# A mixture-of-experts kernel: routed rows staged one tile ahead, copied by VectorE, with their row numbers copied by GpSimd

## What is computed

```
logits = x @ gate_w.T ; probs = softmax(logits)
topk_w, topk_i = top_k(probs, 2) ; topk_w = topk_w / sum(topk_w)
combine = sum(one_hot(topk_i, 8) * topk_w)
g = x @ w_gate[e] ; u = x @ w_up[e]           # 1024 -> 1408, for each expert e
eo = (silu(g) * u) @ w_down[e]                # 1408 -> 1024
out = sum over e of combine[:, e] * eo
out = out + sigmoid(x @ shared_gate) * shared_expert(x)
```

## Time and profile before

| | |
|---|---|
| three timed runs | 2174.4, 2179.98, 2189.42 us; median 2179.98 |
| the profiled execution | 2164.92 us, its slowest core's span 2163.4 us |
| spans of the eight cores | 2120.9 to 2163.4 us |
| TensorE matmuls busy | 2027.5 us, 94% of the span |
| VectorE, ScalarE, GpSimd busy | 789.7, 559.6 and 223.6 us |
| DMA | 258.35 MB, mean 119 GB/s |
| routed stage on core 7 | 1106.4 us to the end, 38 tiles |

### The profile page before, as it was taken

How to read it: one execution, slowest core, us unless ns; L and a number is a source line. 1 busy time by engine, 2 the same in 40 slices (tenths; PEclk the granted TensorE clock), 3 DMA queues, 4 the chain that set the end, 5 groups by cost and what they waited for, 6 DMA issues and landing times. The chain is left out here.

```text
span 2163.4 us, 37870 instructions; the slowest of 8 cores (2120.9 to 2163.4 us)
## 1 busy us (share of the span) xinstructions
PE 2027.5 (94%) x14227; PEld 1242.7 (57%) x14227; DVE 789.7 (37%) x1945; ACT 559.6 (26%) x967; POOL 223.6 (10%) x197
## 2 busy tenths in 40 slices
PE   6999999966979999999969999999999999999997
PEld 3444444432434444444437777777777767767775
DVE  5677777675325544555311111111111111111111
ACT  1333333321212112211202222223223232222222
POOL 1000000000210111011101111111111111111101
PEclk9999999977989999999989999999999999999999
DMA  9733334465773224322497868778677877777533
GB/s 200 135 99 97 98 98 98 117 131 121 132 200 117 89 109 157 117 89 109 124 182 115 132 105 131 118 115 134 114 128 120 134 112 127 131 111 129 94 54 50
DMA packets 260389, 258.35 MB, mean 119 GB/s; under 512 B 194201, under 2 KB 200604, under 8 KB 258082
## 3 DMA queue, kind: packets, MB, share of 16 engines
q0 software_dynamic: 55440, 140.28, 38.2%
q1 hardware_dynamic: 204818, 116.36, 21.8%
HBM read 219.65 MB, written 83.49 MB: 140 GB/s over the span
## 5 line engine op out<-in xcount | busy, mean ns | idle before, releaser
L1364 PE MATMUL ffn_ps<-r_xT,w 128*128 128x256 bf16 (+1 forms) x6688 | 687.3, 265 | 31.4 <-PEq L1198 31.4
L1364 PEld LDWEIGHTS ffn_ps<-r_xT,w 128*128 128x128 bf16 x6688 | 613.1, 98 | 109.8 <-issue 36.4
L1294 DVE TENSOR_TENSOR r_h<-r_si,ffn_ps 128x256 bf16<-128x256 bf16 (+1 forms) x418 | 165.9, 400 | 875.8 <-DVEq L1198 874.1
L1073 PE MATMUL ffn_ps<-xln2T,w 128*128 128x512 bf16 x1408 | 307.0, 380 | 2.5 <-DVE sh_h L1086 2.5
L1274 ACT ACTIVATE r_si<-ffn_ps 128x256 bf16<-128x256 f32 (+1 forms) x418 | 151.8, 367 | 425.5 <-ACTq L1198 422.7
L394 PE MATMUL att_ps<-xlnT,w 128*128 128x512 bf16 x1024 | 237.8, 382 | 1.2 <-DVE xlnT L348 1.1
L1073 PEld LDWEIGHTS ffn_ps<-xln2T,w 128*128 128x128 bf16 x1408 | 136.8, 98 | 166.0 <-issue 4.6
L1322 POOL DMA_INDIRECT out<-r_y,r_meta x70 | 111.0, 1586 | 695.0 <-POOLq L1198 657.9
L1374 PE MATMUL ffn_ps<-w,r_h 128*128 128x512 bf16 x770 | 169.3, 379 | 0.0
L1374 PE MATMUL ffn_ps<-xca,r_h 128*128 128x512 bf16 x770 | 169.3, 379 | 0.0
L394 PEld LDWEIGHTS att_ps<-xlnT,w 128*128 128x128 bf16 x1024 | 96.0, 98 | 116.0 <-issue 4.6
(11 more groups left out here) (152 smaller groups left out, 1121.1 us busy)
## 6 DMA issues: line engine op xcount, KB each, us to landing
xca<-x SPq DMA_DIRECT2D x48, 512.0 KB, 5.7
w<-wu POOLq DMA_DIRECT2D x16, 1408.0 KB, 13.3
w<-wg POOLq DMA_DIRECT2D x8, 2112.0 KB, 15.2
combT_d<-cb SPq DMA_DIRECT2D x8, 1024.0 KB, 4.9
x1b<-x SPq DMA_DIRECT2D x16, 512.0 KB, 5.2
out<-xca SPq DMA_DIRECT2D x16, 512.0 KB, 3.4
out<-x1b SPq DMA_DIRECT2D x16, 512.0 KB, 3.7
xca<-wd POOLq DMA_DIRECT2D x4, 2048.0 KB, 14.4
```

The costliest lines, as they stand in the source:

```text
L1073: i = q.matmul(b_, wslot[w][:, dt * IFF + it * C:dt * IFF + (it + 1) * C], xT2[t % 2][:, dt, :], start=(dt == 0), stop=(dt == 7))
L1294: v.tensor_mul(h[:, it, 0:rt], rsi[:, it % 4, 0:rt], bank(2 + it % 4)[:, RT:RT + rt]).then_inc(r_h, 1)
L1364: i = q.matmul(bank(2 + it % 4)[:, c0:c0 + rt], w_[:, dt * IFF + it * C:dt * IFF + (it + 1) * C], xT[:, dt, 0:rt], start=(dt == 0), stop=( ...
```

## The change

The rows are loaded into a new buffer `r_xTn`. VectorE copies it to `r_xT` at the start of each of its tiles, frees the new buffer (xfree) and tells TensorE with a new semaphore (xr). TensorE waits for xr and no longer frees anything. GpSimd copies the 128 row numbers of a half into a small buffer `r_ids` before each indirect DMA, which reads its numbers there; so meta is freed as soon as both DMAs are issued, ahead of the waits for their landing. In SBUF `r_xTn` takes the place that `r_xT` had, a buffer `r_skip` that nothing uses keeps `r_y` clear of `x1b`, and ScalarE's wait for the stores is gone. The tile sizes are as before.

```diff
@@ -1182,16 +1182,19 @@
         dn_done = (v_dn.h, v_dn.n)
         wout_done = wpe
 
-    xT = sb2("r_xT", [C, 8, RT], BF16)
+    xTn = sb2("r_xTn", [C, 8, RT], BF16)
     h = sb2("r_h", [C, NIT, RT], BF16)
     rsi = sb2("r_si", [C, 4, RT], BF16)
     meta_f = sb2("r_meta", [C, 2, (ROW - D) // 2], F32)
+    r_skip = sb2("r_skip", [C, 5 * D + 256], F32)
     ysb = sb2("r_y", [C, 2, D], F32)
+    xT = sb2("r_xT", [C, 8, RT], BF16)
     meta_i = meta_f[:, :, :].bitcast(I32)
-
-    r_xfull, r_xfree, r_gu, r_si, r_h, r_y, r_yfull, r_yfree, r_mfull, r_mfree, r_expert = (
+    ids = sb2("r_ids", [C, 2], I32)
+
+    r_xfull, r_xfree, r_xr, r_gu, r_si, r_h, r_y, r_yfull, r_yfree, r_mfull, r_mfree, r_expert = (
         es.enter_context(nc.semaphore("r_" + k)) for k in
-        ("xfull", "xfree", "gu", "si", "h", "y", "yfull", "yfree", "mfull", "mfree", "expert"))
+        ("xfull", "xfree", "xr", "gu", "si", "h", "y", "yfull", "yfree", "mfull", "mfree", "expert"))
     acc = [[sem("r_acc%d_%d" % (hf, e)) for e in range(8)] for hf in range(2)]
 
 
@@ -1215,7 +1218,7 @@
 
 
     def first_rows(s):
-        s.dma_start_transpose(out=xT[:, :, :], in_=dr["xs"].bitcast(BF16)[0:RT, 0:D]
+        s.dma_start_transpose(out=xTn[:, :, :], in_=dr["xs"].bitcast(BF16)[0:RT, 0:D]
                               ).then_inc(r_xfull, 16)
         s.dma_start(out=meta_f[:, :, :], in_=dr["xs"][0:RT, D // 2:ROW // 2].rearrange(
             "(b p) c -> p b c", p=C)).then_inc(r_mfull, 16)
@@ -1255,7 +1258,7 @@
         with s.Fori(1, total, 1):
             r = s.snap(row, min_val=0, max_val=8 * REG - RT)
             take(s, r_xfree)
-            s.dma_start_transpose(out=xT[:, :, :], in_=dr["xs"].bitcast(BF16)[bass.ds(r, RT), 0:D]
+            s.dma_start_transpose(out=xTn[:, :, :], in_=dr["xs"].bitcast(BF16)[bass.ds(r, RT), 0:D]
                                   ).then_inc(r_xfull, 16)
             take(s, r_mfree)
             s.dma_start(out=meta_f[:, :, :], in_=dr["xs"][bass.ds(r, RT), D // 2:ROW // 2].rearrange(
@@ -1265,7 +1268,6 @@
 
     def act_routed(a):
         wait(a, cnt_tok)
-        wait(a, out_stored[1])
         a.sem_inc(r_yfree, 1)
         for e, n, full in expert_tiles(a):
             def tile(rt):
@@ -1289,6 +1291,9 @@
         wait(v, cnt_tok)
         for e, n, full in expert_tiles(v):
             def tile(rt):
+                take(v, r_xfull, 16)
+                v.tensor_copy(xT[:, :, :], xTn[:, :, :]).then_inc(r_xfree, 1)
+                v.drain().then_inc(r_xr, 1)
                 for it in range(NIT):
                     take(v, r_si)
                     v.tensor_mul(h[:, it, 0:rt], rsi[:, it % 4, 0:rt],
@@ -1319,9 +1324,11 @@
 
             def add_rows(hf, i):
                 take(g, r_yfull)
+                g.tensor_copy(ids[:, hf:hf + 1], meta_i[:, hf, 0:1])
+                g.drain()
                 g.indirect_dma_start(
                     out=dr["out"],
-                    out_offset=bass.IndirectOffsetOnAxis(ap=meta_i[:, hf, 0:1], axis=0),
+                    out_offset=bass.IndirectOffsetOnAxis(ap=ids[:, hf:hf + 1], axis=0),
                     in_=ysb[:, hf, :], in_offset=None, compute_op=ALU.add
                 ).then_inc(acc[hf][e].h, 16)
 
@@ -1332,9 +1339,10 @@
                     add_rows(0, i)
                     with g.If_ne(half, i):
                         add_rows(1, i)
+                    g.sem_inc(r_mfree, 1)
+                    with g.If_ne(half, i):
                         g.wait_ge(acc[1][e].h, 16 * (i + 1))
                     g.wait_ge(acc[0][e].h, 16 * (i + 1)).then_inc(r_yfree, 1)
-                    g.sem_inc(r_mfree, 1)
                     g.reg_sub(left, left, 1)
                     next_part(e, i + 1)
             for i in range(2, 4):
@@ -1355,7 +1363,7 @@
             wg, wu, wd = wslot[sl], wslot[sl + 1], wslot[sl + 2]
 
             def tile(rt):
-                take(q, r_xfull, 16)
+                take(q, r_xr)
                 for it in range(NIT):
                     if it >= 4:
                         take(q, r_h)
@@ -1375,8 +1383,6 @@
                                          h[:, it, hf * C:(hf + 1) * C],
                                          wd[:, it * D + dc * 512:it * D + (dc + 1) * 512],
                                          start=(it == 0), stop=(it == NIT - 1))
-                            if hf == 0 and dc == 0 and it == 0:
-                                i.then_inc(r_xfree, 1)
                         i.then_inc(r_y, 1)
             tile_loop(q, n, full, tile)
     em("tensor", pe_routed)
```

## The result

| | before | changed |
|---|---|---|
| median of the timed runs | 2183.18 us (4 runs) | 2238.28 us (4 runs) |
| ratio, paired on one chip | | 1.0187, 95% interval 1.0124 to 1.0249 |
| the profiled execution | 2164.92 us | 2232.96 us |
| again on a second chip (`e2_again`) | | 2232.68 us, ratio 1.0238 (1.0179 to 1.0296) |

What follows compares the result with a forecast made beforehand. TensorE was taken as the bound, its idle time in the routed stage as winnable. -17.2 - 16.5 + 0.5 + 1.7 + 0.5 = -31.0 us takes the median 2179.98 to 2149 us, range 2135 to 2168.

Steps and rivals of the forecast that it cites:

- what is added: Costs of the change: VectorE's copy +0.5 us, clock behind the first gap +1.7, GpSimd's copy and drain +0.5.
- H+3.7: H is a half tile's start; GpSimd was to release meta (mfree) about 3.7 us after it.
- Rival 3: GpSimd's copy and drain dear, c us per copy, delaying meta and row loads: 2196 us at c = 7; chance 0.03.
- The first wait: TensorE's 15.45 us wait in the first routed tile goes, with 1.72 us of clock: -17.2 us.
- what is late next: With the first wait gone, the second tile's rows, issued about 1123, arrive by the need at about 1134.
- The small waits: TensorE's waits behind full and half tiles (4.7 and 8.3 us) and 5.0 of clock go, 1.5 stay: -16.5 us.
- VectorE's copy: Copying r_xTn to r_xT takes 1.26 us, hidden in 37 tiles, exposed in the first: +0.5 us, 0 to 1.
- Clock behind the first gap: After the 3.2 us gap before the first routed tile, core 7 may pay a lower clock: +1.7 us, 0 to 1.7.
- The sum: All terms on core 7: -31.0 us, from the median 2179.98 to 2149 us.
- Rivals 1, 2 and 4: After half tiles waits stay (2158 to 2167, 0.15); stage start transfer-bound (2154 to 2160, 0.11); ScalarE's wait merely replaced (2166, 0.04).

Runs made afterwards that it cites:

- e9_wait: The changed kernel with a semaphore in place of GpSimd's drain, and ScalarE's wait for the last stores put back: 2164.68 us, ratio 0.9948.
- e1_sem: The changed kernel, with a semaphore after GpSimd's copy of the row numbers in place of the drain: 2149.21 us, ratio 0.9899.
- e4_store: The kernel before, with only the results' staging moved and ScalarE's wait for the stores taken out: 2178.33 us, ratio 1.0012.
- e5_noids: The changed kernel without the row numbers' copy and drain, meta freed after both DMAs have landed as before: 2179.94 us, ratio 1.0005.
- e6_act: The changed kernel without GpSimd's copy and drain; ScalarE copies the row numbers and frees meta: ratio 0.9873.
- e10_late: e1_sem with one GpSimd drain added for each tile, behind the waits for both landings: ratio 0.988.
- e3_drain: The kernel before with only a GpSimd drain added ahead of each indirect DMA, no copy: 2261.59 us, ratio 1.0414.

## Why the prediction was wrong, step by step

**The step that failed** is the last entry of "what is added": "GpSimd's copy of 128x1 and a drain before each of 70 scatters", priced at +0.5 us, 0.1 to 1.5, with the remark that 69 cost nothing but what they add to H+3.7. The copy was priced rightly (0.18 us). The drain was priced as a sequencer's instruction, from the row of a MEMSET and that of a scatter's issue, neither of which has a drain in it: the bound from both sides held no row of the thing bounded. It took 0.3 to 14.7 us. The profile of the kernel before did hold a row of the thing itself, which neither the numbered rows nor the prediction shows. Between the attention and `emit_ffn` all engines meet (L59), GpSimd right behind two weight loads. Its two drains at that line on core 7 (the other is the program's last), and the second load:

```profile
L59 POOLq DRAIN  x2: 3789/23270/42752, 452.9 to 2159.3; - x2
...
w<-swu POOLq DMA_DIRECT2D x1, 2816.0 KB, 41.9
```

The drain of 42.75 us ended at 495.6 and the load, issued at 453.3, had landed at 495.2. On all eight cores the drain ended 0.46 or 0.47 us after the load had landed. Of the numbered rows, the weight part of 23.9 us in the earlier trace rows gave the upper bound to ask about.

**Rival 3** named the mechanism: mfree late, and with it meta and transpose. Its price for c = 7 was 2196 us; measured were 2238, and by the ratio 2180 x 1.0187 = 2221. It was short because c isn't one number. A weight part ahead makes it 14 (and the drains themselves moved that part up to the half tile), two drains stand in series in a full tile, and then waits appear behind full tiles too (4.17, 3.55). Its chance was 0.03; the row that was to speak against it, a MEMSET, does not speak of a drain at all.

**The first wait**, -17.2: right. It is gone in all kernels without it that stage ahead, and `e9_wait` against `e1_sem` measures 19.6 and 16.1 us on the two cores. The argument for what is late next (second tile's rows at 1123 against a need at 1134) held for the second buffer. `e4_store` shows that without the buffer nothing would have been won, and `e5_noids` that without an early release of meta a wait of 8 to 13 us comes back before the third tile.

**The small waits**, -16.5: right in kind, a little large. In `e1_sem` none stands behind a half tile, where 1.5 us were left for them. Of the three behind full tiles two are gone; the one before the tile that begins at 1881.40 stays:

```profile
1881.40 21.04 PE L1373 MATMUL ffn_ps<-r_xT,w 128*128 128x256 bf16 x176 [2.06 <-PEq L1202]
```

In the kernels that stage ahead without the drain the same tile waits 1.7 to 3.0 us, and the earlier trace rows has it with 2.58. VectorE had copied the rows by 1872.8, so it isn't for the rows; what it is for stays open. With its clock this is 3.7 us of the sum. `e9_wait` puts the whole term at 10.9 and 12.4 us; on core 7 it would be 12.6 without the 1.7 of clock that this run paid behind its first gap.

**VectorE's copy**, +0.5: not paid. In the changed kernel it took 0.71 us in place of 1.26, and the first gap stayed at 2.76 (2.74 before). The line through two rows of other forms was the poor choice. The Trainium skill's 693 ns (VectorE: DVE Perf Modes, The perf-mode tier table) was nearer; the traces agree, with 709 ns in the changed kernel and 694 in `e1_sem`.

**Clock behind the first gap**, +1.7: paid in the changed kernel, `e6_act` and `e10_late` (21.04 us), not in `e1_sem` (19.37) with the same gap of 2.73.

**The sum.** Without the failed step the forecast of -31.0 us stands against -30.5 on core 7 and -28.5 on core 3 (`e1_sem`, routed stage), a median of 2149.21 us, and by the ratio 2180 x 0.0101 = 22 us less. That the first of these meets the forecast within a microsecond is in part luck. The first wait with its clock was the 17.2 us of the sum. The small waits gave 2.3 us less than the sum has, but 2.2 us for the two entries above weren't paid. The down matmuls, which the sum leaves out, took 1.3 us less. And the tail, from TensorE's last matmul to the end, grew by 2.3 us (13.2 to 15.6) where the sum has 0.5; why so much stays open.

Rivals 1, 2 and 4 didn't occur: no wait behind half tiles in `e1_sem`, the second tile starts at once, and the first tile runs through in the changed kernel.

## What to carry to other kernels

Before a drain is put into an engine's stream, ask what that engine has in flight, its DMAs included, and reckon with the landing of the longest; wait for the one result with a semaphore instead. Look for the same instruction on the same engine anywhere in the trace, also far from the stage that is changed. When one queue serves several buffers in order, a second buffer for one of them is worth nothing until the releases ahead of it in the queue come early as well: here the second row buffer and the dropped store wait gave nothing without the row numbers' copy (1.0005), the dropped store wait gave nothing alone (1.0012), and all three together gave 1.0%. A row that bounds a new instruction must contain it or something that waits for the same things.

## What the runs showed of the hardware

- A drain on GpSimd lasted until the DMAs that GpSimd had issued were in memory: 6.3 us in the median of 70 and 14.7 at most in the changed kernel (core 7), 42.75 us in the kernel before behind a load of 2.8 MB that took 41.9. Where none was in flight it took 0.1 to 0.4 us, with two exceptions whose cause stays open: the first drain of the routed stage took 5.95 us (`e3_drain`) or 6.11 (`e10_late`), and the drain at the end of the program 3.8 us in the kernel before and in `e1_sem`, but 0.13 in the changed kernel, whose routed stage is full of drains.
- A transposing load issued by SyncE did not hold a drain on GpSimd up: 35 of the 37 short drains of `e10_late` on core 7 ran while one was in flight.
- GpSimd's copy of 128x1 took 0.18 us alone, but 0.8 when it began while the scatter ahead was still being issued (the rows at 1252.64 and 1268.01), which makes the group's mean 0.39.
- A wait of 2.7 us on TensorE was followed by a slow tile in some executions and not in others, on the same core with the same gap (21.04 us in `e6_act`, 19.37 in `e1_sem`).
